# A third layer's norm chain for chunk 0, moved from inside the scan's last chunk to behind it

## The reference

```python
x = x + _layernorm(block(_layernorm(x, axis=-1), ...), axis=-1)
```

```python
q = concat([q * c, q * s_]); k = concat([k * c, k * s_])
def step(S, inp):                              # over the positions of the sequence, here 2048
    S = jnp.exp(lt)[..., None] * S + kt[..., None] * vt[..., None, :]
    return (S, jnp.einsum('bhe,bhev->bhv', qt, S))
g = o * jax.nn.sigmoid(x @ wg1 @ wg2)
rms = jnp.sqrt(jnp.mean(gg * gg, axis=-1, keepdims=True) + EPS)   # per head
return (gg / rms).reshape(b, n, d) * norm_w @ wo
```

## Time and profile before

| | us |
|---|---|
| runs: median, lowest, highest | 1163.33, 1161.24, 1166.98 |
| the profiled execution: its time | 1164.01 |
| its span, first to last instruction | 1162.2 |
| busy: PE, DVE, ACT, POOL | 952.9, 832.0, 653.1, 647.8 |
| first and last scan of layer 2 (line 2231) start at | 208.2, 313.5 |
| first product with q and last (line 1808) start at | 210.7, 315.4 |

### The profile page before, as it was taken

The page is one execution under the profiler, slowest core; times in us unless marked ns, Lnnn a source line. Parts: engine busy times, 40 slices in busy tenths (PEclk is TensorE's granted clock), DMA queues, the critical chain, the costliest instruction groups (busy, mean ns, idle before and its releaser), DMA issues.

```text
span 1162.2 us, 11517 instructions
## 1 busy us (share of the span) xinstructions
PE 952.9 (82%) x2997; PEld 555.2 (48%) x2997; DVE 832.0 (72%) x1110; ACT 653.1 (56%) x1188; POOL 647.8 (56%) x454
## 2 busy tenths in 40 slices
PE   6879885788899742999999999875878777874996
PEld 3324332233367432788888888431323232352884
DVE  4995348999855474666666666588999999654664
ACT  5756666102366631555555555778666666362555
POOL 3030135788821221777777777305999999341772
PEclk9979997899999966999999999987989899986999
DMA  2000200000020003666666666000000000003651
GB/s 77 1 0 1 87 35 15 0 1 0 0 68 1 21 0 68 150 138 159 141 155 145 150 150 149 2 0 0 1 0 1 0 1 0 15 7 63 142 129 37
DMA packets 18645, 61.29 MB, mean 53 GB/s; under 512 B 2560, under 2 KB 12416, under 8 KB 12800
## 3 DMA queue, kind: packets, MB, share of 16 engines
q1 hardware_dynamic: 18608, 60.86, 22.2%
HBM read 59.15 MB, written 1.70 MB: 52 GB/s over the span
## 4 chain that ended last, share of the span: by engine, by line
PE 40%; DVE 18%; POOL 11%; issue 8%; ACT 3%; DMA 2%; POOLq 0%; SPq 0%; DVEq 0%; ACTq 0%
PE ps L469 39%; POOL g L1845 7%; DVE g L2231 4%; DVE g L1873 3%; DVE y L2509 2%; ACT rstd L1124 1%; DVE g L2465 1%; DVE tmp L1873 1%; DMA g<-coef_scratch 1%; DVE resid L1873 1%; POOL tmp L1854 1%; POOL rstd L1854 1%; ACT g L1124 1%; DVE g L2509 1%; DMA coef_scratch<-g 1%
## 5 line engine op out<-in xcount | busy, mean ns | idle before, releaser
L469 PE MATMUL ps<-parts 128*128 128x512 f32 x1704 | 419.6, 406 | 26.9 <-DVE g L1873 11.4
L469 PEld LDWEIGHTS ps<-parts 128*128 128x128 f32 x1704 | 326.9, 193 | 115.6 <-DVE g L1873 12.3
L1774 POOL TENSOR_TENSOR parts<-g,parts 128x512 fp32r<-128x512 f32 x168 | 217.9, 1297 | 159.2 <-ACT parts L1124 155.3
L1124 ACT ACTIVATE g<-ps 128x512 f32<-128x512 f32 (+3 forms) x290 | 171.3, 596 | 202.4 <-PE ps L469 173.9
L469 PE MATMUL ps<-g,arena 128*128 128x512 f32 (+2 forms) x408 | 193.5, 615 | 34.9 <-POOL g L1808 15.1
L1873 DVE TENSOR_TENSOR ps<-g,ps 128x512 f32<-128x512 f32 x168 | 116.9, 696 | 109.1 <-PE ps L469 87.1
L1845 POOL TENSOR_TENSOR g<-g 128x1024 f32<-128x1024 f32 x64 | 149.1, 2361 | 51.1 <-DVE g L1873 50.7
L1873 DVE TENSOR_TENSOR g<-ps,g 128x512 f32<-128x512 f32 (+1 forms) x164 | 115.5, 704 | 41.9 <-DMA g<-coef_scratch 15.6
L469 PEld LDWEIGHTS ps<-g,arena 128*128 128x128 f32 (+1 forms) x408 | 77.2, 198 | 142.9 <-issue 87.6
L1124 ACT ACTIVATE parts<-g 128x512 fp32r<-128x512 f32 (+2 forms) x252 | 126.3, 533 | 34.1 <-DVE g L1873 17.2
L1124 ACT ACTIVATE ps<-g,small 128x512 f32<-128x512 f32 x131 | 85.1, 682 | 50.5 <-DVE g L2509 29.5
(11 more groups left out here) (188 smaller groups left out, 1072.4 us busy)
## 6 DMA issues: line engine op xcount, KB each, us to landing
g<-coef_scratch SPq DMA_DIRECT2D x80, 512.0 KB, 6.2
g<-in_moe_dram SPq DMA_DIRECT2D x42, 192.0 KB, 4.7
g<-in_rope_dram SPq DMA_DIRECT2D x1, 2048.0 KB, 9.0
arena<-in_weights_dram SPq DMA_DIRECT2D x1, 1348.5 KB, 5.6
arena<-in_weights_dram SPq DMA_DIRECT2D x1, 1028.5 KB, 4.8
g<-in_x_dram SPq DMA_DIRECT2D x4, 256.0 KB, 3.9
out_dram<-g SPq DMA_DIRECT2D x4, 256.0 KB, 2.5
arena<-in_weights_dram SPq DMA_DIRECT2D x1, 838.0 KB, 7.0
```

The source lines that it names most:

```text
L469: return nc.tensor.matmul(o, lhsT, rhs, start=start, stop=stop, **kw)
L1124: return nc.scalar.activation(o, i, func, **kw)
L1774: pv.tensor_tensor(hid_lo[:, cols(c)], g[:, 6, (c % 2) * N:(c % 2 + 1) * N], hid_hi[:, cols(c)].bitcast(F32), ALU.subtract).then_inc(s["hl ...
```

## The change

On all four engines the work of the tail stands behind the loop of the scan. Within the loop only spread_v, sum_heads, inputs, the scans, the products and the copies are left, with signs1 and signs0 at copy 23. On TensorE sum_heads(31) comes first behind the loop, then the roots and wo(0), wo(1) in the order of ROOTS. No instruction is added or taken out.

```diff
--- before.py
+++ after.py
@@ -864,24 +864,18 @@
             for k in range(8 * CHUNKS):
                 if k + 3 < 8 * CHUNKS:
                     spread_v(k + 3)
-                if k == 26:
-                    wo(0)
-                if k == 31:
-                    wo(1)
                 if k:
                     sum_heads(k - 1)
-                if k == 24:
-                    root_of("rms", 2, 0)
-                if k == 26:
-                    root_of("post", 2, 0)
-                if k == 28:
-                    root_of("rms", 2, 1)
-                    root_of("rms", 2, 2)
-                if k == 29:
-                    root_of("pre", 3, 0)
+            sum_heads(8 * CHUNKS - 1)
+            root_of("rms", 2, 0)
+            wo(0)
+            root_of("post", 2, 0)
+            root_of("rms", 2, 1)
+            root_of("rms", 2, 2)
+            root_of("pre", 3, 0)
+            wo(1)
             root_of("post", 2, 1)
             wo(2)
-            sum_heads(8 * CHUNKS - 1)
             root_of("post", 2, 2)
             for m in range(4):
                 first(0, m)
@@ -1442,14 +1436,13 @@
                 f(v_copy(k), ps[:, v_bank(k), :], ACT.Copy).then_inc(s["v_copied"], 1)
                 if k == 23:
                     signs1()
-                    rms_square(0)
-                if k == 27:
-                    rstd_back("rms", 2, 0)
                     signs0()
-                    post_square(2, 0)
-                    rms_square(1)
-                    rstd_back("post", 2, 0)
-                    rms_square(2)
+            rms_square(0)
+            rstd_back("rms", 2, 0)
+            post_square(2, 0)
+            rms_square(1)
+            rstd_back("post", 2, 0)
+            rms_square(2)
             rstd_back("rms", 2, 1)
             rstd_back("rms", 2, 2)
             rstd_back("pre", 3, 0)
@@ -1811,8 +1804,7 @@
                             k = 8 * c + e + 3
                             if k % 4 == 3 and k < 8 * CHUNKS:
                                 features_in(k)
-                            if 8 * c + e == 28:
-                                square_of_x(2, 0)
+                    square_of_x(2, 0)
                     input_lo(0, 0)
                     square_of_x(2, 1)
                     square_of_x(2, 2)
@@ -2231,17 +2223,12 @@
                     last = v.tensor_tensor_scan(state, fast_decay(c), two_of(0, 11, k)[:, r, :],
                                                 state[:, N - 1:N] if c else 0.0, ALU.mult, ALU.add)
                 last.then_inc(s["st_ready"], 1)
-                if k == 23:
-                    gated_out(0)
-                    gated_out(1)
-                if k == 25:
-                    rms_scaled(0)
-                if k == 26:
-                    gated_out(2)
-                if k == 28:
-                    add_back(2, 0)
-                if k == 30:
-                    rms_scaled(1)
+            gated_out(0)
+            gated_out(1)
+            gated_out(2)
+            rms_scaled(0)
+            add_back(2, 0)
+            rms_scaled(1)
             h_back(3, 0)
             rms_scaled(2)
             add_back(2, 1)
```

## The result

The changed kernel takes 1176.34 us (median of 4 runs, 1175.67 to 1177.46) against 1163.61 for the kernel before: the ratio is 1.0108, with a 95% interval of 1.0081 to 1.0135. Slower by 12.7 us; 1177 had been forecast, with a range of 1171 to 1183.

A forecast was written before the change was run, and what follows sets the result against it. It took TensorE (40% of the chain of waits) as the bound, with any delay of the dense stage from 328 us delaying the end. 1164.0 + 10.2 (open chain) + 3.3 (clock) = 1177.5 profiled, median 1177, range 1171 to 1183.

The forecast's parts named there:

- What the scan gets back: VectorE in the third layer's scan: seven instructions leave, 7.2 us back, scans end at 307.5; other end 4.4 us.
- Where the chain starts: TensorE behind the loop: last GpSimd product ends at 311.1, then sum_heads(31), so the rms matmul goes at 312.9.
- The chain's length: Open norm chain behind sum_heads(31): links priced from layers four and five, last logarithm at 332.65, a delay of 10.2 us.
- I therefore take a fall there: TensorE's clock at 314.0 to 318.05: one matmul pair, 1.1 us of 4, so it falls from the 2.4 GHz level.
- the term of 3.3 us for four roots in series: Post 0, rms 1, rms 2 and pre 0 matmuls at the low clock, 0.83 us more each: 3.3 us.
- the list of bounds: Limits of the clock's cost: zero to seven steps, 5.8 us, plus 2.3 for eight two-part matmuls and 1.1 in the last sum_heads.
- the rows of 392 to 396: Clock window in the profile before: 2.02 us of matmul in 4 and the clock stayed up, evidence for no fall.
- A (clock stays up): Rival on TensorE's clock: it never falls, the chain's 10.2 us alone, 1173.5 us; chance 0.25.
- B (down from the loop's end): Rival: clock down from there to the fourth layer's first matmuls, 19.4 us less what comes back, 1182; chance 0.2.
- C (the scan's end decides): Rival, faster: the scan's end and not the chain sets the fourth layer's first matmul, at best 1156.5 us; chance 0.03.
- D (gaps swallow it): Rival, no change: 12.7 us of TensorE gaps in 328 to 412 take up the delay, 1164 us; chance 0.05.
- SyncE's earlier load: Load of layer 4's weights, waiting for sum_heads(31), comes eight microseconds earlier; nothing waits for it at this point.

The follow-up runs named there:

- e6_sum_from_psum: Kernel before, with add_back(2, 0) writing its product back to its PSUM bank and taking the sum into resid from there; 1163.7 us, ratio 1.0002.
- e1_root_first: Changed kernel with root_of("rms", 2, 0) ahead of sum_heads(31) in TensorE's queue; 1171.4 us, ratio 1.0064 to before.
- e3_filled: Changed kernel with ten more matmuls that nobody reads, set in TensorE's waits (PSUM bank 7); 1171.5 us, ratio 1.0072 to before.
- e2_signs_early: Changed kernel with signs2 moved back under the scan, behind signs0; 1171.4 us, ratio 1.0064 to before.
- e4_rms_inside: Changed kernel with gated_out(0) to (2), rms_scaled(0), rms_square(0) and the rms root inside the scan again; 1177.1 us, ratio 1.0113 to before.
- e5_pre_behind: Kernel before with only add_back(2, 0), square_of_x(2, 0) and the pre root behind the loop, after sum_heads(31); 1168.7 us, ratio 1.0047.
- e7_before_filled: Kernel before with four more matmuls that nobody reads in TensorE's waits at the loop's end; 1163.4 us, ratio 0.9996.

## Why the prediction was right

**What the scan gets back**: 7.2 us, measured 7.3 (106.5 to 99.2). The price in place was the right one; e6_sum_from_psum shows that the dear part of add_back was a wait for GpSimd's product. The Trainium skill, "SBUF — State Buffer", section "Who interferes with whom", says that a VectorE instruction with two SBUF inputs contends with a GpSimd instruction that reads SBUF, and the trace agrees with 2.36 against 0.69 us for one instruction at one place.

**Where the chain starts**: the rms root was put at 312.9 and went at 312.42; TensorE's queue order sets it, as e1_root_first shows by moving it.

**The chain's length**: every link went 0.4 to 0.9 us sooner than forecast, of which 0.4 is the earlier start of the scan in this execution (wo(0) 316.15 forecast, 315.61 measured; the pre root 323.8, 323.35; h_back 326.35, 325.86; the post root of chunk 2 331.5, 330.65). In all the post root of chunk 2 came 9.7 us later, counted from the first scan, instead of 10.1 (10.2 at its logarithm). Behind the last product stood 3.3 us of chain up to that root before and 20.1 now, and the product came 7.2 earlier: 16.8 less 7.2 gives this delay, but for rounding. That four roots share one bank shows in waits of 0.87 us behind the logarithm before, as at 323.35.

**The clock**: right that it falls and near in what it costs, wrong in where, and the nearness is luck. The step that failed is "I therefore take a fall there", for 314.0 to 318.05, and with it the term of 3.3 us for four roots in series. The window of 313.5 to 317.5 had 1.21 us of matmul in 4, less than the 1.71 ahead of the fall in the kernel before, and the clock held. All four roots ran at the high clock (1.10 to 1.13 us each), and between 317 and 325, where 0.5 to 0.8 was forecast, the granted clock was 1.00. It fell at about 329, behind the wait of 2.23 us in which signs2 stands. The 3.3 us were not paid; 2.5 were, in the post root of chunk 2 (2.08 instead of 1.02 to 1.12) and the eight two-part records (4.28 instead of 2.41), both in the list of bounds and not in the sum. e3_filled takes them away with fillers alone. The sum had 0.4 us too much for the chain and 0.8 too much for the clock, and the profiled execution took 1175.67 us against 1177.5; that the median lies within 0.7 of the forecast owes something to chance. The reading also took one execution for a rule: the rows of 392 to 396, where the clock "stayed up", belong to the stretch in which it fell in seven of the eleven profiles. So with sparse activity the clock may fall, and the numbers of one trace did not say in which gap. The Trainium skill, "TensorE: Matmul & The Clock Gate", Part 1, says that activity is what releases the throttle; e3_filled agrees, with 1.00 against 0.50 in the same window.

**The rivals**: A (clock stays up) is what the profile of e3_filled shows, 9.7 us at second(0, 0), and with signs2 away that of e2_signs_early. B (down from the loop's end) is out: the clock read 1.00 up to 329 us, and the delay was 12.1 and not 19.4, though its half-speed first matmuls did come. C (the scan's end decides) is out: scans ended 7.3 us earlier, and the layer behind them began 9.9 later (10.3 counted from the first scan). D (gaps swallow it) is out: the distance was 12.1 at second(0, 0) and 12.6 at the experts. SyncE's earlier load did no harm: the window of 313.5 to 317.5 has a DMA share of 0.76, and the wait from square to root at 317.42 is 0.69 us, as at 330.65 with no DMA.

## What to carry to other kernels

In this kernel, work that stood between two iterations cost the busy engine its own length; behind the loop it cost the latency of every engine that it passed through. 7.3 us of one queue stood against 16.8 us more of chain: from the last product to the post root of chunk 2 it was 3.3 us before and is 20.1 now (310.54 to 330.65). The first half of the chain could stand on either side (e4_rms_inside); the last links, on which the next stage waits, could not (e5_pre_behind). And a small fixed job such as signs2 was free only as long as its queue had slack around it. A fall of the clock that one profile shows or lacks is one case only: look at several profiles before a forecast rests on it.

## What the runs showed of the hardware

Where TensorE's clock fell in a chain of single matmuls, it cost more than on the links: it also hit the first matmuls of the dense stage behind it (4.28 and, in e5_pre_behind, 4.10 us against 2.41 for eight records). With ten filling matmuls in the gaps the granted clock read 1.00, the 2.4 GHz level, where it had been 0.50, and no link was delayed. Whether the clock falls in a sparse stretch changed from one profile to the next: behind the same three waits near 400 us it held in four profiles and fell in seven. Removing one stall can create another between VectorE and GpSimd: when the last product came in time (e7_before_filled), a VectorE product with two SBUF operands grew from 0.68 to 2.83 us.
